# Four stages of a transformer sandwich as one program: no meeting of the engines between stages, each engine's line in stage order

## The chip, the core and the metric

The kernel runs on one core of a Trainium2 chip. The core has five engines that run their own instruction lines and meet only through semaphores: TensorE (PE in the profile; PEld is its weight load), VectorE (DVE), ScalarE (ACT), GpSimd (POOL) and SyncE (SP), which here only starts DMAs. An engine takes its instructions strictly in the order in which they were written for it; an instruction that waits holds up all that stand behind it on the same engine. The metric is the time of one execution in microseconds (us) on the device, as a median of several.

## What is computed

The input x has 16 batches of 256 rows by 128 columns, fp32. Four stages, each with a layer norm ahead and behind and a residual sum, run one after the other over all of it:

```python
x = x + ln(_L0_attn_ref(ln(x), ...))   # A: causal attention, 16 heads of 8, low-rank weights, then an MLP
x = x + ln(_L0_ffn_ref(ln(x), ...))    # B: dense MLP plus experts found by two top-8 searches
x = x + ln(_L1_attn_ref(ln(x), ...))   # C: causal attention, 16 heads of 8
x = x + ln(_L1_ffn_ref(ln(x), ...))    # D: 6 layers of local attention (window 32) and a gated MLP
```

Stage D is by far the longest: six layers, each over 32 tiles of 128 rows.

## The kernel before

**Layout.** x stays in SBUF the whole time (XR), and a second copy (XX) holds stage D's running value. One tensor, `arena`, holds all of SBUF and is cut by hand; later stages use the same columns again. PSUM is cut into four slots of 1024 columns (`ps0` to `ps3`).

**Pieces and places.** Each stage is a function (`phase_attention` for A and C, `phase_b`, `phase_d`) that describes a batch as some 40 to 60 small pieces (such as `st0`: statistics; `n0`: normalize; `h`: transpose; `hT`: copy out of PSUM; `q0`, `q1`: the Q and K products of stage D). A table `PLACE` gives each piece a place in thousandths of a batch's period. A piece of batch b has the key 1000 b + place, and each engine emits its part of all pieces in the order of the keys. So the batches are pipelined, and the order on every engine is fixed beforehand.

**Joining of stages.** `together` (line 228) takes several stages and sorts their pieces, for each engine apart, by a time that the stage's `clock` makes of the key. Stage A is run by itself, B is emitted by its own loops, and C and D are given to `together` as a pair: C has the clock (0, 19.1 us a batch), D (346, 14.78 us a tile), each with an offset for each engine. Put into numbers: C's last pieces come at 335 (PE), 332 (ACT), 339 (DVE) and 349 (POOL), D's first real ones at 345 on PE and ACT and later on the others. So only D's piece `early` (key -4000) stands inside C's line, on DVE at 287 and on POOL at 300 (C's batch 13). On POOL `early` clears the borders of three shifted-input buffers (line 1767), signals `zeroed`, and builds the first rotary tables (lines 1722 and 1723). The first thing that D does on ACT, `xs` of batch 0 (line 1562), waits for `zeroed`.

**Meetings.** `Core.fence` (line 192) makes PE, ACT, DVE and POOL drain, and all five engines wait until all four have done so. It is called at the start of B and at the start of C. Stage beginnings stand right behind it: in B the product of two weight matrices on PE (`sim`, line 974), its copy on ACT (line 1062) and two casts on POOL; in C six memsets on POOL for each of which a set of buffers waits (lines 787 to 790, three sets), then `n0` of batch 0 on POOL (line 264 to 272). SP passes the second meeting too and then issues stage D's twelve weight loads.

**PSUM slots.** In A, C and D a use of a slot goes to the slot whose present use ends first by the clock (`Slots`); in B the four slots are taken in turn (`Banks`). A use waits until the one before it in its slot has been copied out.

Names for the steps below: in A the last pieces are `m2` (line 511, PE), `r3` (line 264/266, POOL) and `xr` (line 759, DVE). In B `st0` (254 to 258, DVE), `r0` (264 to 1184, POOL), `n0` (1000, ACT), `spA`/`spB` (958/959, PE) and their copies `spcA`/`spcB` (1020, ACT), `mxA`/`mxB` (1091, DVE) open a batch; `xr` (1187, POOL) closes it. In C `n4` (264 to 272, POOL) closes a batch. In D `sh` (1454, PE), `xs` (1562, ACT), `q0`/`q1` (1368/1369, PE), `sq0`/`sq1` (1508, ACT), `ro0`/`ro1` (1627/1628, DVE) open a tile.

Of the kernel before, what the change touches and what calls it, by code (L numbers as in the profile page):

```python
# [68 lines left out]

class Signal:  # L70


    def __init__(self, name, handle, base):
        self.name, self.h, self.base, self.n = name, handle, base, 0
# [9 lines left out]
    def at(self, n):  # L84
        assert n > 0, (self.name, n)
        return self.h, self.base + n

    def now(self):
        return self.h, self.base + self.n


class Banks:


    def __init__(self, n):
        self.n, self.uses, self.place = n, [], {}

    def take(self, use):
        self.place[use] = len(self.uses)
        self.uses.append(use)  # L100

    def slot(self, use):
        return self.place[use] % self.n

    def before(self, use):
        i = self.place[use] - self.n
        return self.uses[i] if i >= 0 else None
# [20 lines left out]
class Core:  # L128
# [4 lines left out]
    def __init__(self, nc, d, ctx):  # L133
# [6 lines left out]
        self.spare, self.held, self.made = [], [], 0  # L140
        self.psum, self.holders = None, {}
        self.phase_end, self.phases = ctx.enter_context(nc.semaphore("phase_end")), 0
# [17 lines left out]
    def give(self, signals):  # L160
        self.spare += [(x.h, x.base + x.n) for x in signals if x]

    def signals(self, *names, without="", apart=False):
        if not apart:
            self.give(self.held)
            self.held = []
        names, S = " ".join(names).split(), []
        for name in names:
            if name in without.split():
                S.append(None)  # L170
                continue
            if not self.spare:
                self.spare.append((self.ctx.enter_context(self.nc.semaphore(f"s{self.made}_{name}")), 0))
                self.made += 1
            h, base = self.spare.pop(0)
            S.append(Signal(name, h, base))
        self.held += [x for x in S if x]
        return namedtuple("Signals", names)(*S)

    def loads(self, names):  # L180

        names = names.split()
        return namedtuple("Loads", names)(*[Signal(n, self.ctx.enter_context(self.nc.semaphore(n)), 0) for n in names])
# [25 lines left out]
def plan(units, order):  # L209


    out, todo, live, k = [], sorted(units, key=lambda u: u[0]), [], 0
    while live or todo:
        while todo and todo[0][0] <= k:
            live.append(todo.pop(0))
        for u in sorted(live, key=lambda u: order[u[1]][k - u[0]]):
            out.append((u[1], k - u[0], u[3]))
            if k - u[0] + 1 == u[2]:
                live.remove(u)
        k += 1  # L220
    return out


Stage = namedtuple("Stage", "order when takes programs")


def together(C, stages):
# [3 lines left out]
    C.psum = Slots(4)  # L231
    for e in range(5):
        line = sorted(((st.when[e](x[0]), i, x) for i, st in enumerate(stages) for x in st.order), key=lambda y: y[0:2])
        if e == 0:
            for _, i, x in line:
                stages[i].takes(*x)
# [38 lines left out]
def phase_attention(C, K, V, first):  # L275
# [9 lines left out]
    if not first:  # L285
        C.fence()
# [1839 lines left out]
```

## Time and profile before

| | us |
|---|---|
| median of 3 runs | 4243.88 (4242.3 to 4247.86) |
| the profiled execution | 4240.87 |
| its span, first to last instruction | 4239.5 |
| PE busy | 3830.5 (90%) |
| DVE busy | 3339.7 (79%) |
| ACT busy | 3333.3 (79%) |
| POOL busy | 2871.4 (68%) |

The whole execution in 40 slices of 106 us, busy tenths, with the granted TensorE clock in tenths:

```profile
PE   7888456656887999999999999999999999999998
DVE  5765998983656988888888888888888888888884
ACT  4665788884554889888888888888888888888885
POOL 1221888873445888777777777777777777777773
PEclk9999777788998999999999999999999999999999
```

The first four slices are stage A (PE ahead), the next five or so are B (DVE, ACT and POOL ahead, PE at half), three are C, and from the thirteenth on it is D, in which PE is never below nine tenths until the last slice. The borders between stages are the dips.

### The profile page before, as it was taken

Reading aid. Unit: us, or ns where it says so; the run is one execution under the profiler, and the core shown is the slowest. Engines: PE = TensorE matmul, PEld = TensorE weight load, DVE = VectorE, ACT = ScalarE, POOL = GpSimd, SP = SyncE. Lnnn points to the kernel's source line nnn. Section 1 sums busy time; section 2 is a strip of 40 time slices with the busy share of each in tenths; the row PEclk is TensorE's granted clock in tenths of the full one; section 3 lists DMA queues with packets and bytes.
Section 4 is the critical chain, followed back from the end, with each engine's and each line's share of the span. In section 5 each row is a group of like instructions: output and inputs, shape, how many; then the busy total and the mean of one; then the engine's idle time right before and its main releaser. Section 6 shows DMA issues by size and latency. Waiting matters only on the chain.

```text
span 4239.5 us, 149245 instructions
## 1 busy us (share of the span) xinstructions
PE 3830.5 (90%) x62848; PEld 3015.2 (71%) x62848; DVE 3339.7 (79%) x6090; ACT 3333.3 (79%) x5141; POOL 2871.4 (68%) x2624
## 2 busy tenths in 40 slices
PE   7888456656887999999999999999999999999998
PEld 5666345545664677777777777777777777777787
DVE  5765998983656988888888888888888888888884
ACT  4665788884554889888888888888888888888885
POOL 1221888873445888777777777777777777777773
PEclk9999777788998999999999999999999999999999
DMA  2000000000000111111111111111111111111111
GB/s 67 3 3 2 1 1 1 1 1 30 3 3 3 32 27 26 38 31 26 26 36 34 24 28 25 38 31 27 25 37 34 24 28 25 36 22 26 28 25 38
DMA packets 191912, 96.89 MB, mean 23 GB/s; under 512 B 167888, under 2 KB 180880, under 8 KB 191120
## 3 DMA queue, kind: packets, MB, share of 16 engines
q1 hardware_dynamic: 191248, 87.34, 9.2%
q8 instruction: 502, 8.22, 0.8%
q14 instruction: 162, 1.33, 0.1%
HBM read 23.89 MB, written 2.10 MB: 6 GB/s over the span
## 4 chain that ended last, share of the span: by engine, by line
PE 75%; ACT 7%; POOL 6%; issue 6%; DVE 5%; POOLq 0%; ACTq 0%; DVEq 0%
PE ps L1432 16%; PE ps L1420 9%; PE ps L1368 8%; PE ps L1369 8%; PE ps L1398 7%; PE ps L1377 4%; PE ps L1409 3%; PE ps L1486 3%; PE ps L1467 3%; PE ps L1475 3%; PE ps L415 2%; PE ps L1388 1%; ACT arena L584 1%; PE ps L464 1%; PE ps L390 1%
## 5 line engine op out<-in xcount | busy, mean ns | idle before, releaser
L1732 POOL TENSOR_TENSOR arena<-arena 128x1024 f32<-128x1024 f32 x384 | 910.6, 2371 | 27.7 <-DVE arena L1628 22.1
L1751 POOL TENSOR_TENSOR arena<-arena 128x1024 f32<-128x1024 f32 x192 | 365.3, 1902 | 593.8 <-DVE arena L1656 593.8
L1738 POOL TENSOR_TENSOR arena<-arena 128x1024 f32<-128x1024 f32 x384 | 726.8, 1903 | 5.1 <-ACT arena L1524 5.0
L1432 PEld LDWEIGHTS ps<-arena 128*128 128x128 f32 x6144 | 713.5, 192 | 20.6 <-issue 3.2
L1432 PE MATMUL ps<-arena 128*128 128x128 f32 x6144 | 717.1, 275 | 0.0
L1627 DVE TENSOR_TENSOR arena<-ps,arena 128x1024 f32<-128x1024 f32 x384 | 468.2, 1219 | 193.6 <-ACT arena L1508 192.9
L1628 DVE TENSOR_TENSOR arena<-ps,arena 128x1024 f32<-128x1024 f32 x384 | 465.9, 1213 | 0.0
L264 POOL TENSOR_SCALAR arena<-arena 128x2 f32<-128x2 f32 x256 | 73.4, 287 | 573.8 <-DVE arena L258 562.8
L1636 DVE TENSOR_REDUCE arena<-arena 128x32 f32<-128x2048 f32 x192 | 436.9, 2275 | 0.2 <-issue 0.2
L1368 PE MATMUL ps<-arena 128*128 128x512 f32 x768 | 415.2, 622 | 3.0 <-DVE arena L1628 1.9
L1534 ACT ACTIVATE arena<-ps 128x1024 f32<-128x1024 f32 x192 | 196.8, 1025 | 279.5 <-PE ps L1409 279.5
L1420 PE MATMUL ps<-arena 64*128 64x256 f32 x3072 | 401.0, 394 | 3.0 <-DVE arena L1628 1.5
L1508 ACT ACTIVATE arena<-ps 128x1024 f32<-128x1024 f32 x384 | 389.0, 1014 | 12.3 <-PE ps L1369 9.8
L1369 PE MATMUL ps<-arena 128*128 128x512 f32 x768 | 393.7, 594 | 0.0
L1540 ACT ACTIVATE arena<-ps 128x1024 f32<-128x1024 f32 x384 | 374.0, 1038 | 4.1 <-PE ps L1420 4.1
L1398 PE MATMUL ps<-arena 64*32 64x64 f32 x24576 | 334.1, 224 | 4.8 <-issue 4.7
L966 PE MATMUL ps<-arena 128*128 128x128 f32 x1024 | 177.2, 353 | 172.2 <-POOL arena L1243 172.2
L1420 PEld LDWEIGHTS ps<-arena 64*128 64x128 f32 x3072 | 279.5, 187 | 59.4 <-ACT arena L1534 47.2
L1398 PEld LDWEIGHTS ps<-arena 64*32 64x32 f32 x24576 | 299.6, 105 | 29.4 <-issue 5.8
L966 PEld LDWEIGHTS ps<-arena 128*128 128x128 f32 x1024 | 171.1, 265 | 187.4 <-POOL arena L1243 187.4
L1369 PEld LDWEIGHTS ps<-arena 128*128 128x128 f32 x768 | 146.7, 191 | 185.6 <-issue 185.6
L1377 PE MATMUL ps<-arena 64*128 64x64 f32 x6144 | 261.0, 223 | 12.0 <-POOL arena L1738 7.4
(251 smaller groups left out, 8737.1 us busy)
## 6 DMA issues: line engine op xcount, KB each, us to landing
arena<-arena SPq DMA_DIRECT2D x96, 256.0 KB
arena<-arena SPq DMA_DIRECT2D x480, 32.0 KB
arena<-in_dWqk SPq DMA_DIRECT2D x12, 512.0 KB, 5.7
arena<-arena SPq DMA_DIRECT2D x96, 64.0 KB
arena<-arena SPq DMA_DIRECT2D x96, 63.5 KB
arena<-in_dWvT SPq DMA_DIRECT2D x6, 512.0 KB, 4.2
arena<-in_dWo SPq DMA_DIRECT2D x6, 512.0 KB, 4.8
arena<-arena SPq DMA_DIRECT2D x192, 0.2 KB
```

The costliest lines, as they stand in the source:

```text
L1368: pe.matmul(p[:, 0:512], xs, w[:, 0:512], start=True, stop=True)
L1369: pe.matmul(p[:, 512:1024], xs, w[:, 512:1024], start=True, stop=True).then_inc(*qk_ps[g].up())
L1377: i = pe.transpose(p[:, 512 * blk + 64 * c:512 * blk + 64 * c + 64], a1[half, 128 * c:128 * c + 128], ident[half, half])
L1398: i = pe.matmul(p[32 * blk:32 * blk + 32, 512 * bank + 64 * c:512 * bank + 64 * c + 64], qT[half, c, 32 * blk:32 * blk + 32], kT[half, c, ...
L1420: i = pe.matmul(p[:, 512 * u:512 * u + 512].rearrange("p (c b q) -> p c b q", c=8, b=2)[:, :, blk, :], w[half, k % 2, 2 * g + blk, :], pT[ ...
L1432: i = pe.matmul(p[:, 0:128], o[:, u, c, :], w[:, u, c, :], start=(u == c == 0), stop=(u == 1 and c == 7))
L1508: act.activation(SQ[:, 1024 * g:1024 * g + 1024], ps(f"q{g}", n), ACT.Square).then_inc(*sq[g].up())
L1627: dve.tensor_tensor(o1, p.rearrange("p (h e) -> p h e", h=16), bc(cs, 1, 16), ALU.mult)
L1628: dve.tensor_tensor(o2, p.rearrange("p (h u e) -> p h u e", h=16, u=2)[:, :, ::-1, :], bc(sn.rearrange("p (u e) -> p u e", u=2), 1, 16), A ...
L1636: dve.tensor_reduce(SC[n % 3][:, :, 0], SQ.rearrange("p (h e) -> p h e", h=32), AX.X, ALU.add).then_inc(*S.step_dve.up())
L1732: pool.tensor_tensor(a1[:, half], a1[:, half], T2[:, half], ALU.add).then_inc(*radd[g].up())
L1738: pool.tensor_tensor(a3, a3, bc(ss[:, 16 * g:16 * g + 16], 2, 64), ALU.mult).then_inc(*nrm[g].up())
```

## The change

All four stages are handed to `together` in one call, and `fence` is gone. The lines of the engines are no longer sorted by a clock: `weave` puts a later stage's pieces behind, or by a list of turns between, those of the stages before. Here all lists of turns are empty, so each engine's line is all of A, all of B, all of C, all of D.

What follows from it in the code:

- Stage beginnings become pieces named `begin` with the lowest key of their stage, so they stand behind the last piece of the stage before on the same engine. D's `early` stands behind C's last piece too.
- In the place of a meeting stand single waits for the last use of a buffer (`before`, `earlier`): B's first `spcA`, `spcB`, `upc`, `n1` on ACT and `st0` on DVE wait for A's `pp`, `outd` or `xra` of batch 15; C's `st0` waits for B's `xr` of the same batch, its `begin` for B's `ot` of batch 14, its first exponentials for `ot` of batch 15; D's `early` on DVE and its loads on SP wait for B's last `xr` and `ot`.
- SBUF is cut anew: A's weights and B's late buffers lie above column base + 25736, so that the beginning of a stage doesn't lie on what the stage before still uses. Sizes and numbers of buffers are the same.
- All four stages share one `Slots`, by clocks in `TIMES`; B no longer takes slots in turn.
- Some loads share a semaphore, so the first user waits for the group (for instance stage A's `ld_b12` for four small loads).

```diff
+TIMES = {"a": [[-6000, 0], [0, 15], [16000, 373]], "b": [[-6000, 385], [0, 400], [16000, 930]], "c": [[-6000, 955], [0, 975], [16000, 1281]], "d": [[-9000, 1270], [0, 1290], [10000, 1438]]}
+TURNS = [[[], [], [], [], []], [[], [], [], [], []], [[], [], [], [], []]]
...
-    def fence(self):
-
-        self.phases += 1
-        engines = (self.pe, self.act, self.dve, self.pool)
-        for e in engines:
-            e.drain().then_inc(self.phase_end, 1)
-        for e in (*engines, self.sp):
-            e.wait_ge(self.phase_end, 4 * self.phases)
...
+def weave(line, later, turns):
+
+    out, done = line[:len(line) - sum(turns[1::2])], 0
+    for n, m in zip(turns[0::2], turns[1::2]):
+        out += later[done:done + n]
+        done += n
+        at = len(out) - done
+        out += line[at:at + m]
+    return out + later[done:]
...
+        line = [(0, x) for x in stages[0].order]
+        for i, st in enumerate(stages[1:]):
+            line = weave(line, [(i + 1, x) for x in st.order], turns[i][e])
+        lines.append(line)
...
             if piece in ("spcA", "spcB"):
+                if b == 0:
+                    act.wait_ge(*(before.outd if t else before.pp_ps).at(NB))
+                if b == 1:
+                    act.wait_ge(*(before.xra if t else before.outd).at(NB))
...
-    bufs = Banks(4)
-    bufs.take(("sim", 0))
...
+    due, tag = clock(*TIMES["b"]), "b"
+    empties = {"h": "hT", "up": "upc", "spA": "spcA", "spB": "spcB", "atA": "atcA", "atB": "atcB", "ot": "n1"}
...
-    tag, when = "d", clock(346, 14.78, (59, 103, 17, -905, 59))
-    due = when[1]
+    order = [(-9000, "begin", 0, 0)] + order
+    tag, due = "d", clock(*TIMES["d"])
...
+        A = phase_attention(C, K, la, True)
+        assert C.top <= K.base + 25736
+        B = phase_b(C, K, lb, A.S)
+        c = phase_attention(C, K, lc, False, A.S, B.S)
+        ld = load_d(C, [*la.L, *B.S[63:]])
+        D = phase_d(C, K, ld, DEPTH, out, B.S[:63], c.S, B.S)
+        together(C, [A, B, c, D], TURNS)
```

## Rows read from the trace of the kernel before

**Rows 1.** Busy time by stretch: PE, PEld, DVE, ACT, POOL, granted clock, DMA share, GB/s

```profile
409.40:1000.50 591.10, 349.82 (x1840) 288.37 (x1840) 497.27 (x1728) 478.93 (x1472) 457.74 (x627) 0.78 0.00 1
...
1334.80:1420.00 85.20, 62.52 (x1029) 38.58 (x1030) 74.94 (x80) 53.47 (x64) 74.81 (x52) 0.84 0.10 26
1420.00:4239.50 2819.50, 2800.32 (x47931) 2224.45 (x47929) 2332.07 (x3085) 2395.52 (x2945) 2130.03 (x1573) 1.00 0.13 29
```

**Rows 2.** Timeline, all engines, border of A and B: start, us, operation, idle before

```profile
400.49 3.94 PE L511 MATMUL ps<-arena 128*128 128x128 f32 x32
...
407.52 0.71 POOL L266 TENSOR_TENSOR arena<-arena 128x2 f32<-128x2 f32 x1
...
408.90 0.42 DVE L759 TENSOR_TENSOR arena<-arena 128x256 f32<-128x256 f32 x1
...
409.43 3.67 PE L974 MATMUL ps<-arena 64*128 64x64 f32 x16 [5.00 <-DVEq L197]
...
411.71 0.24 POOL L1184 TENSOR_SCALAR arena<-arena 128x2 f32<-128x2 f32 x1
413.20 0.60 ACT L1062 ACTIVATE arena<-ps 128x512 f32<-128x512 f32 x1 [10.88 <-PE ps L974]
413.69 0.48 ACT L1000 ACTIVATE arena<-arena 128x128 f32<-128x128 f32 x1
```

**Rows 3.** Timeline, first tile of B: its two products and their copies

```profile
419.41 1.65 PE L958 MATMUL ps<-arena 128*128 128x512 f32 x2
...
419.66 1.02 ACT L1020 ACTIVATE arena<-ps 128x1024 f32<-128x1024 f32 x1 [3.94 <-PE ps L959]
...
421.96 1.02 ACT L1020 ACTIVATE arena<-ps 128x1024 f32<-128x1024 f32 x1 [1.28 <-PE ps L959]
...
423.94 1.09 DVE L1091 MAX8 arena<-arena 128x8 f32<-128x64 f32 x8
```

**Rows 4.** Who PE waited for, 450 to 960 us: us in total, times, longest

```profile
PE ps L966 <- POOL arena L1243: 154.1, 29, 15.8
...
PE ps L946 <- ACT arena L1058: 10.1, 7, 1.5
PE ps L958 <- ACT arena L989: 8.0, 14, 0.8
```

**Rows 5.** Timeline of POOL at the border of B and C

```profile
999.68 0.72 POOL L1187 TENSOR_TENSOR arena<-arena 128x256 f32<-128x256 f32 x1 [0.98 <-ACT arena L1009]
...
1000.57 0.31 POOL L787 MEMSET arena<- 128x256 bf16 x1 [0.17 <-POOLq L197]
```

**Rows 6.** Timeline of POOL: D's `early` inside C, and C's last piece

```profile
1303.10 0.25 POOL L1767 MEMSET arena<- 128x33 f32 x3
...
1303.98 0.74 POOL L1723 TENSOR_TENSOR arena<-arena 128x256 f32<-128x256 f32 x1
...
1342.22 0.80 POOL L272 TENSOR_SCALAR arena<-arena 128x128 f32<-128x128 f32 x1
```

**Rows 7.** Timeline, all engines, the first steps of D

```profile
1334.85 0.38 ACT L1562 ACTIVATE arena<-ps 64x256 f32<-64x256 f32 x1 [1.08 <-PE ps L1455]
...
1335.67 2.08 PE L1368 MATMUL ps<-arena 128*128 128x512 f32 x2 [0.92 <-ACT arena L1563]
...
1339.05 1.02 PE L1368 MATMUL ps<-arena 128*128 128x512 f32 x2
...
1340.38 1.22 DVE L1627 TENSOR_TENSOR arena<-ps,arena 128x1024 f32<-128x1024 f32 x1 [0.18 <-ACT arena L1508]
```

**Rows 8.** Timeline of PE: dense bursts after idle time, for the clock

```profile
975.46 3.84 PE L966 MATMUL ps<-arena 128*128 128x128 f32 x32 [2.83 <-POOL arena L1243]
...
984.59 6.74 PE L966 MATMUL ps<-arena 128*128 128x128 f32 x32 [5.29 <-POOL arena L1243]
...
1358.61 1.97 PE L1377 MATMUL ps<-arena 64*128 64x64 f32 x32 [6.10 <-POOL arena L1738]
...
1362.83 1.02 PE L1369 MATMUL ps<-arena 128*128 128x512 f32 x2
```

More of the change, by code:

```diff
@@ L85, in at @@
         assert n > 0, (self.name, n)
-        return self.h, self.base + n
+        return self.h, self.base() + n
     def now(self):
[L89 to L107, printed above, removed]
+        return self.h, self.base() + self.n
 class Slots:
@@ L158, in sb, with signals @@
         return a
[L160 to L167, printed above, removed]
+    def signals(self, *names, without="", after=()):
+        names, S, after = " ".join(names).split(), [], [x for x in after if x]
         for name in names:
@@ L284, in phase_attention @@
     L, W, Wo, bo, vm = V.L, V.W, V.Wo, V.bo, V.vm
-    if not first:
-        C.fence()
-    C.top = K.base
     S = C.signals(
@@ L308, in phase_attention @@
                        a[:, 512:1536].rearrange("p (c q) -> p c q", c=4)))
-    bz = sb([128, 5])
+    if first:
+        bz, C.edge = sb([128, 5]), C.top
+    C.top = K.base
+    if first:
+        probs = [[sb([128, 3, 4, 128]) for _ in range(4)] for _ in range(2)]
+    else:
+        bz = sb([128, 5])
     sel = V.sel32.bitcast(BF16).rearrange("p (v k) -> p v k", v=4)
@@ L314, in phase_attention @@
                 sb([128, 2, 16]), sb([128, 2, 128])) for _ in range(NS)]
-    probs = [[sb([128, 3, 4, 128]) for _ in range(4)] for _ in range(2)]
+    if not first:
+        probs = [[sb([128, 3, 4, 128]) for _ in range(4)] for _ in range(2)]
+    assert C.top <= K.base + 25736, C.top
     if first:
@@ L580, in unit @@
                 v, s = int(piece[1]), "ab".index(piece[2])
+                if not first and b == 0:
+                    act.wait_ge(*before.ot_ps.at(NB))
                 if b >= 2:
@@ L640, in unit @@
                     dve.wait_ge(*K.ld_x[b // 4].at(16))
+                if not first:
+                    dve.wait_ge(*before.xr.at(b + 1))
                 if not first and b >= NS:
@@ L838, in phase_attention, with phase_b @@
         order = [(-5000 + n, what, 0) for n, what in enumerate(("prep0", "prep1", "prep2"))] + order
-    done = None if first else (S.pp_ps.at(NB), S.x0.at(NB), lambda b: S.x0.at(b + 1))
-    return Stage(order, when, takes, (pe_program, act_program, dve_program, pool_program, sp_program)), done
-def phase_b(C, K, V):
+    order = [(-6000, "begin", 0)] + order
+    return Stage(order, takes, (pe_program, act_program, dve_program, pool_program, sp_program), S)
+def phase_b(C, K, V, before):
     d, sb = C.d, C.sb
@@ new lines, in batch_buffers @@
+    def batch_buffers(up, hT=None):
+        return Batch(stats(C), sb([128, 2]), sb([128, 2, 128]), sb([128, 256]) if hT is None else hT, up)
+    C.top = K.base
+    tiles = [tile_buffers() for _ in range(3)]
+    assert C.top <= K.base + 25736, C.top
+    ups = [sb([128, 4, 256]) for _ in range(2)]
+    hT = sb([128, 256])
+    assert C.top <= K.base + 25736, C.top
+    C.top = K.base + 25736
+    tiles += [tile_buffers()]
+    ups += [sb([128, 4, 256])]
+    late = [batch_buffers(ups[1], hT), batch_buffers(ups[2])]
@@ L990, in batch @@
             if piece == "upc":
+                if b < NU:
+                    act.wait_ge(*(before.xra if b == 2 else before.outd).at(NB))
                 if b >= NU:
@@ L1071, in batch @@
             if piece == "st0":
+                dve.wait_ge(*before.xra.at(NB if b == 2 else b + 1))
+                if b == 1:
+                    dve.wait_ge(*before.outd.at(NB))
                 if b >= NU:
```

405 lines of the change are left out of this document (211 added, 194 removed), and 4 rows, old and new, of the table S.

## The prediction, made before the changed kernel had run

> **What bounds the kernel now.** I read busy time by stage first. From 1420 us to the end, stage D, PE is busy 2800.3 of 2819.5 us at full clock, while DVE, ACT and POOL stay below 86% [rows 1]. So D's long part is worth its PE work and nothing else, and the only thing that a change of borders can do to it is to move its start. In B (409 to 1000 us) no engine is full: DVE 497, ACT 479 and POOL 458 of 591 us, in a ring of waits. A border matters there only if it changes the order on an engine or a PSUM slot that PE waits for. The list of PE's waits inside B has four rows, of which the three that matter here stand in the rows: each names the operand of the waiting product, the sum behind `sg` (line 1243), the copied attention columns (1058), the copied transpose (989); the fourth names the normalized input in the same way [rows 4]. None is a slot that another use still holds.
>
> So I went to the timeline at the three borders, and asked of each which piece of the new stage is last ready, on which engine, and what stands in front of it there in either kernel.
>
> **Border A to B.** Before, PE ends A's last product at 404.43, waits 5.00 us for the meeting, which DVE's `xr` at 408.90 to 409.32 ends, and then runs `sim` (3.67 us). ACT can copy its result only at 413.20, and B's `n0` of batch 0 stands behind that copy, at 413.69. But the statistics that `n0` needs were ready at 411.95 (411.71 + 0.24 on POOL) [rows 2]. So the meeting costs 413.69 - 411.95 = 1.74 us on the path, minus a small gap.
>
> After the change PE goes from `m2` straight to `sim` (404.43 + 3.67 = 408.10), ACT copies it by 408.8, and POOL reaches B's two casts when `r3` ends at 408.23. All that lies beside DVE's last pieces. DVE starts `st0` when `xr` ends, about 0.1 us earlier than behind the meeting, so the statistics are ready at 411.85 and `n0` starts then: 413.69 - 411.85 = **-1.84 us**. The new waits of B for A's last batch (`pp`, `outd`, `xra`) are for events up to 409.32 on instructions that come later than 413, so they hold up nothing; DVE's are for its own earlier work.
>
> The slots add something back. By the clocks of `TIMES`, A's last uses are due at 432, 438, 440 and 462, while B's first are due at 387 to 429. The rule takes the slot that is due first, so `sim`, `h`, `spA`, `spB`, `up` and the second `h` of B all fall on one and the same slot. `spB` then waits for the copy of `spA`, which ends at 420.68, where it now starts at 419.41: 1.3 us later. Its copy ends at 424.3 and not 422.98, and DVE, which comes to it at 423.94, waits about **+0.35 us** [rows 3]. `up` and the second `h` have microseconds to spare. After two batches all slots carry B's own dates. All of B's slots are emptied by ACT in its own order, so taking the one due first is never later than taking them in turn; and since no row of PE's waits names a slot [rows 4], I take 0 for the rest of B. Bounds: above, the two small ones of those rows, 10.1 + 8.0 us, if some of it was a slot after all and goes; below, 1 us of loss.
>
> **Border B to C.** C's path opens on POOL: six memsets and three more, then `n0`. They stand behind B's last `xr` (999.68 to 1000.40) and start at 1000.57 [rows 5]. With no meeting they still stand behind that `xr`, because it is B's last piece on POOL and nothing is woven. Only the gap of 0.17 us goes: **-0.2 us**. DVE's `st0` of C starts some us earlier, which is worth nothing, since `n0` comes behind the memsets on POOL. D's twelve loads are issued about 4 us earlier by SP, which has nothing else in its line; they have over 300 us to land.
>
> **Border C to D.** Here there was no meeting, and by the clocks nothing was woven but `early`. This piece moves. Before, POOL ran it at 1303.10 to 1304.72, inside C, in idle time [rows 6]. After, it stands behind `n4` of batch 15, which ends at 1343.02 (1342.22 + 0.80) [rows 6]. D's first `xs` on ACT waits for it. The three memsets take 0.25 us, so `zeroed` comes at 1343.2, and `xs`, which ran at 1334.85 [rows 7], starts at 1343.3: **+8.45 us**. All of D's first steps hang on it: `q0` at 1335.67, `sq0`, `ro0` on DVE at 1340.38 [rows 7]. C's last pieces on the other engines don't hide it, since DVE and ACT were already waiting for each other at that point (0.18 us idle, released by ACT). The tables (twice 0.74 us [rows 6]) end at 1344.7 and are first read by `ro0`, which is now at 1348.8; DVE's part of `early`, three tiny memsets, lies in DVE's idle time too. If that cover were gone they would cost 1.5 us.
>
> From there to 1420 the ramp is a ring of DVE, ACT and POOL (DVE busy 74.9 of 85.2 us, POOL 74.8 [rows 1]), each step released by the one before; nothing in it is tied to a fixed time, so it shifts as a whole, and PE's full stretch behind it shifts too.
>
> The clock is the open cost. Before, `q0`'s four passes ran at the low clock (3.38 us from 1335.67 to 1339.05), `q1`'s at the high one (2 passes in 1.02 us) [rows 7]. After, PE has been idle for 9.5 us and not 1, and begins `q0` at the low clock as well. How long it stays low under dense work is between two rows: after 10 us with almost no PE work it was low from 1358.61 to 1362.83, and after 5.3 us of idle time a burst of 6.74 us ran low from end to end (an equal one took 3.84 us after 2.8 us of idle time) [rows 8]. `q1` begins 3.4 us into its burst: by the first row about 0.4 us of loss, by the second all of it, 4 x 0.43 = 1.7 us. `xs` of batch 1 and `sq1` stand behind `q1`, and DVE comes to `sq1`'s result with hardly any slack. I take the middle, **+1.0 us**; a gain is excluded, since `q0` was wholly low already.
>
> On this the Trainium skill (TensorE: Matmul & The Clock Gate, What's actually happening) says that the throttled state is the default and that activity releases it. It speaks against this change at this border, since all engines wait for one POOL piece; by it alone `q1` could be wholly low, which is the upper end that the rows give as well.
>
> Stage A's first waits are now for groups of loads. The groups hold neighbours in SP's line, and their first users come behind PE's preparation of the weights; I take 0.
>
> **Sum.** -1.84 + 0.35 - 0.2 + 8.45 + 1.0 = +7.8 us. Against the profiled execution that is 4240.87 + 7.8 = 4248.7 us. That execution lies 3.0 us below the median of the runs; on the median's footing it is 4251.7, and I put **4251.5 us** (+0.18%).
>
> **Rivals.** (1) **The late start of D is taken up in the ramp.** It needs a step between 1343 and 1420 that waits for something which doesn't shift, or slack that closes up. For it speaks that PE is busy only 62.5 of the 85.2 us there [rows 1]; against it, that DVE is full and is released by the pieces that shift. Then only the gains remain, -1.7 us: 4242.2 us on the median's footing.
>
> (2) **Slower: the low clock is met twice.** Later in the ramp PE works in bursts between idle times, and batches of `q0`/`q1` come behind such idle time, on the path of DVE. If the shifted windows leave one more batch of eight passes low, that is 8 x 0.43 = 3.4 us on top of the 1.7 us: 0.7 + 3.4 more than the forecast, +11.9 us, 4255.8 us. It decides against "no change" from one extra group of four passes on.
>
> (3) **Faster: the meetings hid more than the border shows.** If B's list of PE waits did hold slots, 18 us at the most, and the new rule frees them, the sum turns to -10 us, 4233.6 us. Against it stands that each row names the product's own operand.
>
> **How the numbers follow.** Forecast (+6.7 to +8.5 by the clock's bounds, and the runs' own scatter of some 3 us) 0.65; rival 1 0.10; rival 2 0.20; rival 3 0.05. The median of such a kernel can be told from no change from about 0.2% on, 8.5 us. The forecast lies just inside that: I give 0.45 of its 0.65 to "same" and 0.20 to "slower". With rival 1 "same" is 0.55, with rival 2 "slower" is 0.40, "faster" is 0.05. The range 4246 to 4258 takes in the forecast with its scatter and rival 2, and leaves out rivals 1 and 3.
>
> **What would show it.** In the profile after: `n0` of B (line of 1000) about 1.8 us earlier; B's length and the list of its PE waits as now; POOL's memsets in C right behind `xr`; POOL's three small memsets of D behind C's last `n4`, and ACT's first `xs` right behind them, some 8 us after its `sh` on PE; PE idle for 9 to 10 us there; PE's full stretch starting about 7 to 8 us later and lasting 2819 us as now. Wrong would be: an `xs` that doesn't wait for POOL, a B that is shorter or longer by over 2 us, or a stretch of D that takes another time with the same work.

## The result, and the profile after

The changed kernel takes **4252.2 us** (median of 20 runs, 4246.7 to 4261.6) against 4244.7 (20 runs of the kernel before on the same chips): ratio 1.0015, interval 1.0008 to 1.0022, that is +6.4 us (+3.4 to +9.3); the bare difference of the two medians is 7.5. Below, a total in us is the ratio's distance from 1 times the median of the kernel before, with its interval. Forecast were 4251.5 us and +7.8 us. The profiled execution took 4247.38 us, with a span of 4246.0.

A span can be cut at points that both kernels have: the end of A's last sum on DVE, B's first `n0` on ACT, C's first memset on POOL, C's last step on PE (the transposes `sh` with which D begins), D's first `xs` on ACT, D's second `ro0` on DVE, and the start of PE's full stretch. That is the product at 1414.89 us before and 1421.39 after, behind which PE hardly waits until the last tiles of D; the time from `xs` to it is the ramp.

| stretch, us | before | after | difference |
|---|---|---|---|
| A, to the end of its last `xr` | 409.32 | 410.68 | +1.36 |
| to B's first `n0` | 4.37 | 2.49 | -1.88 |
| B, to C's first memset | 586.88 | 583.68 | -3.20 |
| C, to D's `sh` | 333.80 | 336.41 | +2.61 |
| to D's first `xs` | 0.48 | 8.85 | +8.37 |
| to the second `ro0` | 8.26 | 9.02 | +0.76 |
| rest of the ramp, to PE's full stretch | 71.78 | 70.26 | -1.52 |
| full stretch, to the end | 2824.61 | 2824.61 | 0.00 |

The rows with +1.36, -3.20 and +2.61 are lengths of stages whose own work the change doesn't touch. One execution can't tell whether they belong to it; the runs below give their scatter. Together the rows make the 6.5 us between the two profiled executions.

The windows of after, with the columns of [rows 1], are:

```profile
411.00:997.00 586.00, 336.73 (x1824) 273.54 (x1824) 496.98 (x1732) 478.32 (x1472) 463.93 (x625) 0.81 0.01 2
...
1421.00:4246.00 2825.00, 2806.20 (x48030) 2229.19 (x48030) 2338.21 (x3091) 2399.62 (x2949) 2133.42 (x1576) 1.00 0.13 29
```

D's long part is as full as before (2806 of 2825 us) and was only moved. The border of A and B in the timeline of after:

```profile
401.62 3.98 PE L493 MATMUL ps<-arena 128*128 128x128 f32 x32
405.53 2.00 PE L991 MATMUL ps<-arena 64*128 64x64 f32 x16
...
407.56 0.60 ACT L1093 ACTIVATE arena<-ps 128x512 f32<-128x512 f32 x1 [4.07 <-PE ps L991]
...
410.25 0.43 DVE L747 TENSOR_TENSOR arena<-arena 128x256 f32<-128x256 f32 x1
...
412.83 0.24 POOL L1225 TENSOR_SCALAR arena<-arena 128x2 f32<-128x2 f32 x1
413.17 0.49 ACT L1024 ACTIVATE arena<-arena 128x128 f32<-128x128 f32 x1 [5.01 <-POOL arena L1225]
...
420.51 1.10 PE L975 MATMUL ps<-arena 128*128 128x512 f32 x2 [1.26 <-ACT arena L1050]
...
423.62 1.11 DVE L1130 MAX8 arena<-arena 128x8 f32<-128x64 f32 x8
```

`sim` (L991) now stands right behind `m2`, its copy is done long before `xr` ends, and `n0` (L1024) is released by POOL's statistics and no longer held up by the copy of `sim`. `sim` takes 2.00 us, at a granted clock of 1.00, instead of the 3.67 of [rows 2], since PE comes to it from dense work. At 420.51 the wait of `spB` for the copy of `spA` can be seen: both are on one slot. The maxima of the two tiles start at 420.40 and 423.62, 3.22 us apart; before it was 3.23. PE's waits inside B, 450 to 960 us (who PE waited for: us in total, times, longest):

```profile
PE ps L983 <- POOL arena L1284: 165.9, 30, 16.5
PE ps L941 <- ACT arena L1025: 29.4, 14, 2.6
PE ps L963 <- ACT arena L1088: 8.8, 8, 1.6
PE ps L975 <- ACT arena L1011: 7.7, 14, 0.6
```

They are the four of the prediction's list [rows 4], with the same causes, beside 0.3 us of "issue", and none is a slot. POOL at the border of B and C:

```profile
996.19 0.72 POOL L1228 TENSOR_TENSOR arena<-arena 128x256 f32<-128x256 f32 x1 [0.98 <-ACT arena L1035]
996.85 0.31 POOL L782 MEMSET arena<- 128x256 bf16 x1
```

The 0.17 us of [rows 5] is gone, and nothing more. The border of C and D in the timeline of after:

```profile
1333.26 0.27 PE L1502 MATMUL ps<-arena 128*128 128x128 f32 x1
...
1341.10 0.79 POOL L247 TENSOR_SCALAR arena<-arena 128x128 f32<-128x128 f32 x1
1341.83 0.25 POOL L1816 MEMSET arena<- 128x33 f32 x3
...
1342.11 0.38 ACT L1610 ACTIVATE arena<-ps 64x256 f32<-64x256 f32 x1 [9.45 <-POOL arena L1816]
...
1343.02 2.05 PE L1416 MATMUL ps<-arena 128*128 128x512 f32 x2 [9.38 <-ACT arena L1611]
...
1344.86 1.91 PE L1417 MATMUL ps<-arena 128*128 128x512 f32 x2
...
1346.57 1.53 PE L1416 MATMUL ps<-arena 128*128 128x512 f32 x2
...
1351.13 1.22 DVE L1675 TENSOR_TENSOR arena<-ps,arena 128x1024 f32<-128x1024 f32 x1 [0.81 <-ACT arena L1556]
```

D's first `xs` (L1610) waits 9.45 us for the memsets of `early` (L1816), which stand behind C's last `n4` (L247), and PE waits for it. A product `q0` or `q1` is two lines of PE, L1416 and L1417 here, each for one half. `q0` is low in both halves (2.05 and 1.91 us), `q1` in its first (1.53 us); the granted clock from 1343.02 to 1347.94 is 0.54.

### The profile page after: what moved, and what is told of

It reads as the page before. It is cut to its first block, busy times and chain, and to the rows that moved or that the text cites. A ratio compares the mean times of both kernels' runs of the same rounds, so it can differ in the third digit from the quotient of the medians.

```text
span 4246.0 us, 149278 instructions
## 1 busy us (share of the span) xinstructions
PE 3824.4 (90%) x62848; PEld 3003.9 (71%) x62848; DVE 3339.3 (79%) x6090; ACT 3331.8 (78%) x5141; POOL 2875.5 (68%) x2624
## 4 chain that ended last, share of the span: by engine, by line
PE 75%; POOL 7%; ACT 6%; DVE 6%; issue 6%; ACTq 0%; DVEq 0%; POOLq 0%
PE ps L1480 16%; PE ps L1468 9%; PE ps L1416 8%; PE ps L1417 7%; PE ps L1446 7%; PE ps L1425 4%; PE ps L1457 3%; PE ps L1534 3%; PE ps L1515 3%; PE ps L1523 3%; PE ps L397 2%; PE ps L1436 1%; ACT arena L567 1%; PE ps L446 1%; PE ps L372 1%
## 5 line engine op out<-in xcount | busy, mean ns | idle before, releaser
L1480 PE MATMUL ps<-arena 128*128 128x128 f32 x6144 | 717.1, 275 | 0.0
L1416 PE MATMUL ps<-arena 128*128 128x512 f32 x768 | 416.2, 624 | 13.3 <-ACT arena L1611 9.4
L1417 PE MATMUL ps<-arena 128*128 128x512 f32 x768 | 394.0, 595 | 0.0
L983 PE MATMUL ps<-arena 128*128 128x128 f32 x1024 | 167.5, 340 | 174.0 <-POOL arena L1284 174.0
L1417 PEld LDWEIGHTS ps<-arena 128*128 128x128 f32 x768 | 147.0, 191 | 186.9 <-issue 186.9
```

The costliest lines, as they stand in the source:

```text
L1416: pe.matmul(p[:, 0:512], xs, w[:, 0:512], start=True, stop=True)
L1417: pe.matmul(p[:, 512:1024], xs, w[:, 512:1024], start=True, stop=True).then_inc(*qk_ps[g].up())
L1480: i = pe.matmul(p[:, 0:128], o[:, u, c, :], w[:, u, c, :], start=(u == c == 0), stop=(u == 1 and c == 7))
```

## The experiments

My theory was that of the prediction: the delay at C to D passes through undiminished, and the two meetings were worth 2 us. Its rivals were that the ramp takes the delay up, and that the meetings or the slots are worth something else. All kernels are compared with the kernel before in the same session (medians of before: 4246.8 for the first four, 4244.6 for the next four, 4246.8 for the last three), and are numbered as they ran; the ninth stands beside the fifth. The fifth, sixth, eighth, tenth and eleventh ran 5 times, the others 11.

### 1. The late `early` alone, in the kernel before

```diff
-    order += [(-4000, "early", 0, 0), ...
+    order += [(-100, "early", 0, 0), ...
```

> The kernel before with one edit: D's piece early gets the key -100 and so stands behind C's last pieces on POOL and DVE; both meetings stay. My theory (the change lost its time at the border of C and D alone, by this one piece): slower by 6.5 to 8.5 us, the first xs of D some 8.4 us behind where it was, counted from PE's sh, and PE's full stretch as long as before. Rival (the loss comes from the other edits, the single waits, the new SBUF cut or the slots): within 2 us of before. Rival (D's ramp takes the delay up): xs late by 8.4 us, the whole by less than 3 us.

Measured: 4250.8 us, ratio 1.0009 (1.0000 to 1.0018), +3.8 us (0 to +7.6). The first `xs` (timeline of this kernel):

```profile
1345.51 0.38 ACT L1562 ACTIVATE arena<-ps 64x256 f32<-64x256 f32 x1 [9.47 <-POOL arena L1767]
```

That is 8.87 us after `sh` where before has 0.48: +8.39, with both meetings still there. So this one piece makes the whole step at C to D. The second `ro0` came 9.42 us behind `xs`, 1.16 more than before. The total is less than the 6.5 to 8.5 us that I expected, and its interval alone doesn't exclude the second rival, a ramp that takes the delay up; the trace does: from the first `ro0` to the full stretch it took 75.62 us, where before took 74.51.

### 2. The late `early` taken back, in the changed kernel

```diff
-TURNS = [[[], [], [], [], []], [[], [], [], [], []], [[], [], [], [], []]]
+TURNS = [[[], [], [], [], []], [[], [], [], [], []], [[], [], [], [2, 79], []]]
```

This places POOL's `begin` and `early` of D ahead of the last 79 pieces of C.

> The changed kernel with one edit: on POOL the first two pieces of D (its begin, empty there, and early) stand 79 pieces ahead of C's end, where they stood before. My theory: D's first xs follows its sh at once, and the kernel is faster than the one before by what the meetings cost, 1.9 + 0.2 us: -1 to -3 us against before, -8 us against the changed kernel. Rival (the other edits lose time too): still slower than before by 2 us or more.

Measured: 4241.8 us, ratio 0.9988 (0.9979 to 0.9997), -5.1 us (-8.9 to -1.3). The change without its one late piece is faster than the kernel before, where my sum has -1.7 and the steps of this trace make -2.0. `xs` stands 0.48 us behind `sh` again:

```profile
1339.37 0.38 ACT L1610 ACTIVATE arena<-ps 64x256 f32<-64x256 f32 x1 [1.08 <-PE ps L1503]
```

### 3. Both meetings put back, in the changed kernel

```diff
+    def meet(self, e, phase):
+        engine = (self.pe, self.act, self.dve, self.pool, self.sp)[e]
+        if e < 4:
+            engine.drain().then_inc(self.met.h, 1)
+        engine.wait_ge(self.met.h, 16 + 4 * phase)
...
+                if x[1] == "begin" and i in (1, 2):
+                    C.meet(e, i)
...
```

> The changed kernel with a drain and a meeting of the engines put back at the start of B and of C. My theory: n0 of B again 4.3 to 4.4 us behind the start of A's last xr (2.5 us in the changed kernel), POOL's first memset in C 0.2 us later, 2.1 us in all: slower than before by 8.5 to 10 us. Rival (a meeting costs only what its drains take, hidden by A's tail): as the changed kernel, +7 us. Rival (it hid more inside B): slower than the changed kernel by 4 us or more.

Measured: 4251.9 us, ratio 1.0010 (1.0001 to 1.0019), +4.2 us, which can't be told from the changed kernel's time and is less than the 8.5 to 10 us that I expected. The timeline of this kernel at A to B and in B's first tile:

```profile
409.70 3.67 PE L999 MATMUL ps<-arena 64*128 64x64 f32 x16 [5.00 <-DVEq L173]
...
420.09 1.02 ACT L1058 ACTIVATE arena<-ps 128x1024 f32<-128x1024 f32 x1 [4.10 <-PE ps L984]
...
421.26 2.05 PE L983 MATMUL ps<-arena 128*128 128x512 f32 x2 [1.27 <-ACT arena L1058]
...
424.89 1.02 ACT L1058 ACTIVATE arena<-ps 128x1024 f32<-128x1024 f32 x1 [3.77 <-PE ps L984]
```

From the end of `xr` to `n0` it is 4.37 us again, as before, and from the end of B's last `xr` to C's memset 0.24 instead of -0.06. The meetings are worth 1.88 + 0.30 us at their places, and a total can't show that. One thing is new: here the second product, behind its slot, ran at the low clock (2.05 us; granted 0.55 from 421.26 to 424.80), and the two copies stood 4.80 us apart, with DVE waiting 1.49 us for the second.

### 4. B's slots taken in turn, in the changed kernel

```diff
+            turns.append(piece)
-            C.psum.take((tag, piece, b), due(1000 * b + PLACE[empties[piece]]))
+            C.psum.take((tag, piece, b), due(1000 * b + PLACE[empties[piece]]), turn=len(turns))
...
```

> The changed kernel with B's PSUM slots taken in turn again, as the kernel before does, all else as changed. My theory: PE waits for no slot in B either way, so the same time as the changed kernel within 1 us, +7 us against before; only the second product of the first tile starts about 1 us earlier and nothing comes of it. Rival (the slot rule shortened B, which in the changed kernel's profile is some 3 us shorter than before): B is 3 us longer again and the kernel slower than the changed one by 3 us.

Measured: 4252.7 us, ratio 1.0009 (1.0000 to 1.0018), which can't be told from the changed kernel's time. The two copies stand 1.75 us apart instead of 3.22. B took 586.64 us, 3 us more than in after, as the rival has it; but the second experiment, with the changed kernel's rule, has the same 586.64. So the rule for the slots is worth nothing that these runs show.

### The stages' scatter and the ramp

The same cuts through six profiles (us), the first four experiments beside before and after:

| stretch | before | after | 1st | 2nd | 3rd | 4th |
|---|---|---|---|---|---|---|
| A | 409.3 | 410.7 | 408.7 | 413.4 | 409.6 | 413.4 |
| `xr` to `n0` of B | 4.37 | 2.49 | 4.38 | 2.49 | 4.37 | 2.50 |
| B | 586.9 | 583.7 | 587.9 | 586.6 | 587.9 | 586.6 |
| C | 333.8 | 336.4 | 335.7 | 336.4 | 336.3 | 336.5 |
| `sh` to `xs` | 0.48 | 8.85 | 8.87 | 0.48 | 8.84 | 8.87 |
| `xs` to second `ro0` | 8.26 | 9.02 | 9.42 | 8.34 | 9.20 | 9.21 |
| rest of the ramp | 71.8 | 70.3 | 72.0 | 70.3 | 70.3 | 71.7 |
| full stretch | 2824.6 | 2824.6 | 2828.2 | 2826.1 | 2826.6 | 2822.7 |

The steps at the borders repeat to some hundredths. A, B, C and the full stretch scatter by 3 to 6 us each, whatever the kernel; C's 336.4 of after is near what the four others have (335.7 to 336.5), and before's 333.8 is the lowest. The two kernels with the old joining, before and first, do have the two shortest C (333.8 and 335.7), so that some 1 to 2 us of C may belong to the change; that isn't shown. The rest of the ramp takes one of two lengths here, 70.3 or 71.8, with a late start (after, third: the short one; first, fourth: the long one) and without it (second: short; before: long). So the -1.52 in the table of the result isn't the delay being taken up.

The traces show what goes with these lengths: the clock, further on in the ramp. One batch of `q0` and `q1` (at 1372.46 us in before, at 1379.88 in after) takes, from the start of its first line to that of its fourth, 4.61, 5.25 and 5.26 us in before, first and fourth, at a granted clock of 0.57, 0.50 and 0.50, and the next batch starts 10.4, 11.2 and 11.2 us behind it. In second, after and third it takes 3.22, 3.56 and 3.65 us (0.82, 0.74 and 0.72), and the next one starts 9.7 us behind. So a batch met at the low clock does lengthen the ramp, as the prediction's second rival has it, by up to 1.5 us, but in kernels with and without the late start.

### 5. PE kept busy in the gap, first try: the work stood on the path

```diff
+                if n == g == 0:
+                    p = claim(piece, n)
+                    for i in range(56):
+                        pe.matmul(p[:, 0:128], ident, ident, start=True, stop=True, skip_group_check=True)
                 pe.wait_ge(*S.xs.at(m + 1))
...
```

> The changed kernel, and in the 8.7 us in which TensorE waits for D's first strip it multiplies the identity by itself 56 times into the slot of the first product (thrown away by the product itself). If the extra loss behind the late strip is the lower clock alone (rows: the first q products take 2.05, 1.91 and 1.53 us where 1.02 is their time at 2.4 GHz; the second root is 9.13 us later than before against 8.37 of the strip), the first three products take close to 1.02 us each, the second root starts 1.5 to 3 us sooner after the last transposes of C than in the changed kernel, and the time is 0 to 3 us below the changed kernel's. If the late strip costs something else (a slot, an order on ScalarE), the products get faster and the roots don't move. If the ramp that follows is what really sets the start of TensorE's full stretch, the roots move and the full stretch starts no sooner: time as the changed kernel's, 4251 to 4253 against 4246.8.

Measured: 4264.1 us, ratio 1.0046 (1.0032 to 1.0060), +19.5 us. The slot that I took for these products is the one of `sh`, which only the copies `xs` give free, so they ran behind the gap and not in it:

```profile
1346.04 15.18 PE L1415 MATMUL ps<-arena 128*128 128x128 f32 x112 [9.28 <-ACT arena L1615]
```

As a test of the clock it failed. It became a good one of the other question: 15.2 us more on the path at this place made the first `ro0` 13.05 us later than in the changed kernel (27.76 us after `sh` against 14.71), and the time 12 to 13 us longer (by ratio 0.31%). From the first `ro0` to the full stretch it took 73.58 us. In all thirteen profiles of this study that stretch is between 72.97 and 75.62 us, while the first `ro0` stands from 6 to 28 us behind `sh`. So the ramp takes up none of a delay beyond this scatter of 2.7 us.

### 9. PE kept busy in the gap, second try

```diff
+                if n == g == 0:
+                    spare.append(claim("q1", 0))
+                    for i in range(32):
+                        pe.matmul(spare[0][:, 0:128], ident, ident, start=True, stop=True, skip_group_check=True)
                 pe.wait_ge(*S.xs.at(m + 1))
...
```

> The changed kernel, with 32 products of the identity by itself (64 records of a 128x128 product) in the gap before D's first product; this time into the second product's slot, which is free as soon as C's last context transposes are copied, so that they run while TensorE waits for the strip (in the first try they stood behind it: the first product's slot is the one that the strip's copies give free, and 15.2 us of them were added to the path). If the lower clock is what the late strip costs beyond itself, the first products take 1.02 us each where they took 2.05 and 1.91, the second root starts 16 to 17 us behind C's last transposes where the changed kernel has 17.87, and the full stretch 1 to 3 us sooner; the time 1 to 3 us below the changed kernel's, that is 0 to 0.15% above the kernel before. If the clock doesn't rise in the gap, no change. That the ramp takes the gain back: roots sooner, full stretch not.

Measured: 4256.1 us, ratio 1.0022 (1.0013 to 1.0032). The timeline of this kernel:

```profile
1335.32 9.21 PE L1417 MATMUL ps<-arena 128*128 128x128 f32 x64
...
1343.80 0.38 ACT L1616 ACTIVATE arena<-ps 64x256 f32<-64x256 f32 x1 [9.97 <-POOL arena L1822]
...
1344.71 1.10 PE L1422 MATMUL ps<-arena 128*128 128x512 f32 x2 [0.17 <-ACT arena L1617]
...
1345.64 1.02 PE L1423 MATMUL ps<-arena 128*128 128x512 f32 x2
```

With PE busy through the gap the two halves of `q0` take 1.10 and 1.02 us, not 2.05 and 1.91 (granted clock 1.00 from 1344.71 to 1348.00), and the second `ro0` stands 6.75 us behind `xs` instead of 9.02. So the low clock costs 2.27 us there in the changed kernel. In the kernel before it costs less than 8.26 - 6.75 = 1.51, because there DVE is still busy with C's last unit: in the sixth experiment, below, where `early` isn't late and `q0` ran at the full clock, the second `ro0` stands 7.79 us behind `xs`, so about 0.5 us of before's 8.26 is the clock. The full stretch began 86.62 us behind `sh`, 1.51 sooner than the changed kernel's 88.13, but the total doesn't show it: the interval overlaps that of the change and its middle, +9.3 us, lies above it and above the 0 to 0.15% that I expected. The profile has the loss in the full stretch, 2833.3 us, the longest of all, with 8.2 us of waits by the name of "issue" (below). Whether the filler causes that I can't tell.

### 6. C's head ahead of B's tail

The timelines of both kernels show PE waiting 11 us at B to C for POOL. In the timeline of before it is

```profile
1007.60 0.45 PE L429 MATMUL ps<-arena 128*128 128x128 f32 x1 [11.49 <-POOL arena L272]
```

and in the timeline of after, with B's last product and C's next one:

```profile
988.82 3.81 PE L963 MATMUL ps<-arena 128*128 128x128 f32 x32 [0.95 <-ACT arena L1088]
...
1003.76 0.47 PE L411 MATMUL ps<-arena 128*128 128x128 f32 x1 [11.14 <-POOL arena L247]
...
1004.92 1.22 PE L418 MATMUL ps<-arena 128*128 128x256 f32 x2 [0.47 <-ACT arena L542]
```

What the change did not use is that pieces of the next stage may stand in front of the last ones of this stage. Two edits beside the second experiment's: the turns, and the memsets behind the first normalization.

```diff
+TURNS = [[[], [], [], [], []], [[], [9, 5], [5, 6], [2, 6], []], [[], [], [], [2, 79], []]]
...
                     normalize(pool, ...).then_inc(*S.pn0.up())
+                    if b == 0:
+                        clear()
...
```

`clear` holds the memsets that `begin` had; they are gone from there.

> The changed kernel with the turn of the second experiment at the border C to D, and C's head ahead of B's tail: GpSimd does C's first normalization (and only then its memsets) before the last root and sum of B, VectorE C's first moments before B's last, ScalarE C's first pieces before B's last normalization. If a border costs what TensorE waits for at it, C's first transposes (11.1 us of wait, 996.85 to 1003.76) come 6 to 7.5 us sooner and the time is 8 to 10 us below the kernel before's: 4237 to 4239. If the first units of C only wait further on instead (as B's last output waits now behind them), the first transposes are early, the stretch from B's last output product to the last transposes of C stays within 2 us of the changed kernel's, and the time is that of the second experiment, about 4242 to 4245.

Measured: **4228.3 us**, ratio 0.9961 (0.9948 to 0.9975), -16.6 us (-22 to -11). The timeline of this kernel:

```profile
992.05 3.81 PE L968 MATMUL ps<-arena 128*128 128x128 f32 x32 [0.95 <-ACT arena L1093]
...
995.70 0.27 PE L411 MATMUL ps<-arena 128*128 128x128 f32 x1
...
996.55 0.70 PE L418 MATMUL ps<-arena 128*128 128x256 f32 x2 [0.47 <-ACT arena L542]
...
1321.05 0.38 ACT L1615 ACTIVATE arena<-ps 64x256 f32<-64x256 f32 x1 [1.08 <-PE ps L1508]
...
1321.96 1.10 PE L1421 MATMUL ps<-arena 128*128 128x512 f32 x2 [1.01 <-ACT arena L1616]
...
1328.84 1.21 DVE L1680 TENSOR_TENSOR arena<-ps,arena 128x1024 f32<-128x1024 f32 x1
```

C's first transposes follow B's last product without a wait: 3.65 us from that product's start, where after has 14.94 (988.82 to 1003.76). That is 11.3 us, more than the 6 to 7.5 that I expected, since POOL's normalization stood right behind the piece that releases B's last but one product, and could run under that product. The second experiment's -5.1 us and these 11.3 make -16.4. Of the 11 us some 4 were C's memsets (996.85 to 1000.99 in after), which stood ahead of the normalization; the two edits weren't run apart, so what each is worth alone isn't shown. PE also kept its clock: the next products took 0.70 and 0.59 us where after has 1.22 and 1.06. What the first units of C gained stayed gained: first transposes to `sh` took 324.9 us here, 329.5 in after and 326.8 in before. The last three rows are the start of D named in the ninth experiment: `q0` at the full clock (granted 1.00), and the second `ro0`, which waits for no other engine, 7.79 us behind `xs`.

### 7. B's head ahead of A's tail

```diff
+TURNS = [[[], [], [2, 54], [7, 28], []], [[], [], [], [], []], [[], [], [], [2, 79], []]]
```

> The changed kernel with the turn of the second experiment at C to D, and VectorE's first moments and GpSimd's first root of B ahead of A's last units. If the start of B waits for nothing but this root behind A's last roots on GpSimd, ScalarE's first normalization starts right behind the copy of the keys' product, 5 us sooner, and so do the first copy and maximum of B; the time is 5 us below the second experiment's, 4236 to 4239. If the 1.9 us of the first border showed nothing in the total because B's length takes such gains back, the first maximum is 5 us sooner and the stretch from A's last sum to C's first memset is as long as in the changed kernel (586 to 588 us from the first normalization before) to within 1.5 us: time as the second experiment's.

Measured: 4239.0 us, ratio 0.9985 (0.9976 to 0.9994), against 0.9988 of the second experiment. The timeline of this kernel:

```profile
414.19 1.02 ACT L1050 ACTIVATE arena<-ps 128x1024 f32<-128x1024 f32 x1 [4.10 <-PE ps L976]
...
415.36 2.05 PE L975 MATMUL ps<-arena 128*128 128x512 f32 x2 [1.26 <-ACT arena L1050]
...
419.21 1.02 ACT L1050 ACTIVATE arena<-ps 128x1024 f32<-128x1024 f32 x1 [4.00 <-PE ps L976]
```

The first copy is 5.2 us sooner (after: 419.35). The second product then met its slot and the low clock, so the copies stand 5.02 us apart and of the 5.2 us only 3.4 reached the second maximum. C's first memset stands 585.7 us behind the end of A's last `xr`; it was 586.2 in after and 589.1 in the second experiment, so a trace doesn't settle it either. A total gain of 3 us is inside these intervals, and so is none.

### 8, 10 and 11. All heads, then B's slots, then D's head

The eighth kernel has both sets of turns (ratio in what follows against the kernel before).

> Both of the two before. If the borders add up, 4231 to 4234 (the second experiment's 4243 to 4244 as traces have it, less 5 and less 6 to 7): below the kernel before by 0.25 to 0.35%. If the stages take gains back, no lower than either of the two by 2 us.

Measured: **4226.6 us**, 0.9957 (0.9944 to 0.9971), -18 us, the lowest median of the study; 1.7 us below the sixth, which the intervals don't separate. It lies 4 to 7 us below what I expected, mainly because C's head gave 11.3 us and not 6 to 7; that B's head added anything isn't shown. The tenth also gives B's first four uses a slot each:

```diff
+            turn = {"h": 1, "spA": 2, "spB": 3, "up": 0}.get(piece) if b == 0 else None
+            C.psum.take((tag, piece, b), due(1000 * b + PLACE[empties[piece]]), turn=turn)
```

> The eighth experiment with B's first four pieces on PSUM buffers 1, 2, 3 and 0, so that the second product of B's first tile doesn't wait for the copy of the first. In the seventh experiment, with these products at 1.2 GHz (2.05 and 1.92 us), the two copies stood 5.02 us apart and the maxima 5.01, where the changed kernel has 3.22. If that wait is what takes a part of B's early start back, the two maxima come 3.2 to 3.9 us apart and the time is 1 to 1.8 us below the eighth experiment's 4226.6. If the planner's choice of buffers helped elsewhere, up to 2 us above it.

Measured: 4228.6 us, 0.9955 (0.9941 to 0.9969). The copies stand 1.72 us apart and the maxima 3.22, as expected; the time didn't follow. The eleventh adds D's first product ahead of C's last transposes, `[[7, 8], [4, 7], [], [2, 79], []]` as the last set of turns.

> The one before, with D's first transposes and first product ahead of C's last transposes of the context on TensorE, and its first strip copies ahead of the last context copy on ScalarE. If TensorE's waits in C's last unit are room, the first root of D starts 3 to 5 us sooner after C's last context transposes and the time is 2 to 4 us lower than the one before. If the ramp of D is bound by the root and sum behind it on VectorE and not by when it starts, the time is the same; if C's last unit is pushed back by the product (2 us at 1.2 GHz), it is up to 2 us higher.

Measured: 4228.2 us, 0.9953 (0.9940 to 0.9967), the same. The timeline of this kernel:

```profile
1316.08 2.04 PE L1422 MATMUL ps<-arena 128*128 128x512 f32 x2 [1.01 <-ACT arena L1617]
...
1319.42 0.27 PE L461 MATMUL ps<-arena 128*128 128x128 f32 x1
...
1326.83 1.22 DVE L1681 TENSOR_TENSOR arena<-ps,arena 128x1024 f32<-128x1024 f32 x1
```

The product is early, but DVE comes to the first `ro0` only when its pieces of C's last unit are done, 7.4 us behind C's last context transposes (L461), where I expected 3 to 5 us less than the tenth's 8.4. The product stands 3.3 us ahead of those transposes, where in the tenth it came 3.8 us behind them; of these 7.1 us one reached the root, and none the total.

## Why the prediction was right

The main term, the late `early`, was right in mechanism and size, and it makes the sign and nearly all of the amount. The small terms can't be judged by the total, whose interval is 6 us wide; they are judged by the traces, and two of them were off. That the forecast median came within 1 us of the measured one is in part luck: lengths of stages that nothing in the sum describes moved by +1.36, -3.20, +2.61 and -1.52 us between the two profiles and nearly cancelled.

**A to B, -1.84: right in size and cause.** Measured -1.88, and 4.37 again with the meetings put back. The release changed as written, from the copy of `sim` to POOL's statistics.

**The shared slot at B's head, +0.35: mis-sized, and conditional.** It measured 0 in after: the maxima are 3.22 us apart as before. I had moved the old duration of the product, 1.65 us and partly at the low clock [rows 3], to its new start; it took 1.10, at a granted clock of 1.00, because the clock had risen by the time it started. Where the low clock still held, the same slot cost 1.49 us of DVE's time (third experiment), four times my term. Neither shows in a total.

**The rest of B, 0: right as far as the runs can tell**, by the list of waits and by the fourth experiment. One of my own signs of being wrong did appear, a B that is shorter by over 2 us (-3.20). With the changed kernel's B and nothing woven into it, B took 583.8, 586.1 and 586.6 us in the fifth, ninth and second experiments, against 586.9 and 587.9 in before and first; so the sign was set finer than the scatter of 3 us, and a gain of 1 to 2 us in B is neither shown nor excluded. The 0 for stage A's grouped loads has the same standing: A took 408.7 to 413.4 us in the six profiles of the table, with and without the change.

**B to C, -0.2: right**, -0.23.

**C to D, +8.45: right**, +8.37, and +8.39 when it is the only edit. That DVE's and POOL's other parts of `early` cost nothing is right too.

**The clock, +1.0 (0.4 to 1.7): right in direction and inside its bounds**, +0.76 in after and +1.16, +0.94 and +0.95 in the first, third and fourth experiments, against before's 8.26. Two things in its working were not so. `q0` wasn't wholly low before: it took 3.38 us, and 3.55 in after (its second half 1.68 and 1.91), so it adds 0.17 us of its own; `q1`'s first half adds 0.51 (1.53 us for 1.02), and `q0` began 0.09 us later behind `xs`. And DVE had more room than I gave it: with C's last unit out of its way it could have been 1.04 us sooner at the full clock (6.75 for 7.79), so the clock took that too. The Trainium skill (TensorE: Matmul & The Clock Gate, What's actually happening) has the throttled state as the default that activity releases. The runs agree: useless products in the gap were enough for 1.10 us where 2.05 stood, and the granted clock there went from 0.54 to 1.00.

**The ramp shifts as a whole: right** to within 2.7 us. Rival 1 is refuted by the thirteen profiles with the first `ro0` at 6 to 28 us and the same way, 73 to 76 us, from there to the full stretch. **Rival 2** (a further batch at the low clock) isn't in after's profile, where the rest of the ramp was 1.52 us shorter than before. Its mechanism is real, though: one batch at the low clock makes the ramp 71.8 us and not 70.3 in some profiles, with the delay and without it (in the seven later ones the length is 70.3 to 71.9). That is scatter and not shown to be a cost of the change; in these two profiles it fell on before. **Rival 3** fell with the list of waits.

**The sum.** +7.8 forecast; the border steps of the two traces give -1.88 - 0.23 + 0 + 8.37 + 0.76 = +7.0; the runs say +6.4 (3.4 to 9.3), the bare medians +7.5. The totals of the first experiment (+3.8, at most +7.6, where its steps make +9.5) and the second (-5.1, where they make -2.0) both lie some 3 to 6 us lower than their steps. The third and fourth (+4.2 and +3.8, where their steps make +9.4 and +7.2) do so as well. Between the first and the second the medians differ by 9.0 us and the steps by 11.5, within the intervals of some 4 us each, so most of the shortfall is common to the four; it may lie in the runs of before in that session, which wasn't tested.

**What I missed** was not in the sum. I read the borders for what the change moves there, and so I passed by what PE waits for at them in either kernel: 11 us at B to C, worth more than everything the change does (the rows stand in the sixth experiment).

## What to carry to other kernels

When stages are chained without a meeting, look up for every engine what stands last in the old stage and who waits for the new stage's first piece on it: a piece that had been hidden in idle time, and now stands in stage order, is paid in full (8.4 us for three memsets of 0.25 us in all), while the meetings themselves were worth 2. Both prices are read from the traces; the totals, with their 8 us intervals, only agree with them in part. The gain of one program lies in letting the next stage's head overtake this stage's tail: at the border where TensorE waited 11 us it gave all of that and the clock besides. Where the wait lies behind VectorE's own line, bringing the product forward gives nothing.

## What the runs showed of the hardware

**Waits with nothing behind them in the last stretch.** PE's full stretch, the same instructions every time, took 2822.7 to 2833.3 us. Part of this stands in the list of PE's waits as "issue", time in which PE waited for nothing that the profile shows. From 1400 us to the end, in the fourth experiment and then in the ninth (who PE waited for: us in total, times, longest):

```profile
PE ps L1448 <- issue: 2.4, 2, 2.0
```

```profile
PE ps L1452 <- issue: 7.0, 4, 2.5
PE ps L1422 <- issue: 1.2, 1, 1.2
```

Most of it stands in the same line in both, the 64 small products of the scores; the ninth has 1.2 us before `q0` as well. The longest single stall of all profiles is 3.2 us (eleventh). Over the thirteen profiles the two go together roughly: 2.4 us of such waits with the shortest stretch, 3.2 to 6.3 with those of 2823.4 to 2829.0 us, 8.2 with the longest. From the fourth to the ninth experiment these waits grow by 5.8 us and the stretch by 10.6, so they account for about half of the scatter there. What they are the profile doesn't tell.

**The clock at a border depends on what PE comes from.** `sim` took 3.67 us behind 5.00 us of waiting and 2.00 right behind `m2`; C's first wide products took 1.22 and 1.06 us behind 11 us of waiting (granted clock 0.50), and 0.70 and 0.59 without it (granted 1.00). When such a wait is taken away, this part is gained on top of it.
